# A graph network on one core: order of the fill of its edge loop, and the source one-hots made by VectorE

## What is computed

```python
edge_feat = jnp.concatenate([x[src], x[dst], edge_attr], axis=-1)
h = mish(edge_feat @ W1 + b1)          # W1: (512 + 512 + 64) x 512
messages = mish(h @ W2 + b2)           # W2: 512 x 512
agg = jax.ops.segment_sum(messages, dst, num_segments=x.shape[0])
u = mish(jnp.concatenate([x, agg], axis=-1) @ W3 + b3)
out = u @ W4 + b4                      # then layernorm(x + out) * gamma + beta
```

## Time and profile before

| | |
|---|---|
| median of 3 runs | 254.63 us (254.29 to 255.37) |
| the profiled execution | 255.16 us, of which the trace spans 253.4 us |
| PE, matmuls | 235.5 us busy (93% of the span) |
| VectorE (DVE) | 153.9 us (61%) |
| ScalarE (ACT) | 121.6 us (48%) |
| granted clock of PE, mean | 0.977 of full speed |

### The profile page before, as it was taken

The page is one execution under the profiler, slowest core; times in us unless marked ns, Lnnn a source line. Parts: engine busy times, 40 slices in busy tenths (PEclk is TensorE's granted clock), DMA queues, the critical chain, the costliest instruction groups (busy, mean ns, idle before and its releaser), DMA issues.

```text
span 253.4 us, 3283 instructions
## 1 busy us (share of the span) xinstructions
PE 235.5 (93%) x1269; PEld 189.6 (75%) x1269; DVE 153.9 (61%) x266; ACT 121.6 (48%) x221; POOL 5.6 (2%) x17
## 2 busy tenths in 40 slices
PE   7998999997998499999999999999999998999980
PEld 3967789764765378888888888888888887986760
DVE  3977875336877335585675856758568355264625
ACT  0415399779267614553654735647455343150000
POOL 0000100001000000000000000000000000000001
PEclk9999999999999679999999999999999999999996
DMA  6999983501930000004505031040000000000001
GB/s 214 319 415 414 406 319 132 168 0 35 281 101 0 0 0 0 3 0 134 197 3 166 0 111 60 0 166 0 0 3 0 0 0 0 3 0 0 3 0 43
DMA packets 12991, 23.39 MB, mean 92 GB/s; under 512 B 920, under 2 KB 3888, under 8 KB 12848
## 3 DMA queue, kind: packets, MB, share of 16 engines
q1 hardware_dynamic: 12336, 22.81, 25.7%
q10 hardware_dynamic: 640, 0.37, 0.6%
HBM read 22.92 MB, written 0.26 MB: 91 GB/s over the span
## 4 chain that ended last, share of the span: by engine, by line
PE 82%; DVE 8%; issue 4%; ACT 4%; POOL 1%; POOLq 0%; DVEq 0%
PE bank L625 33%; PE bank L610 12%; PE bank L432 8%; PE bank L441 5%; PE bank L488 4%; PE bank L635 3%; PE bank L636 3%; PE bank L451 2%; ACT C L281 2%; DVE Sbf L829 2%; DVE Dbf L829 2%; PE bank L421 1%; PE bank L646 1%; PE bank L463 1%; PE bank L415 1%
## 5 line engine op out<-in xcount | busy, mean ns | idle before, releaser
L625 PE MATMUL bank<-W2hi,Hhi 128*128 128x512 f32 x128 | 51.1, 399 | 4.2 <-issue 4.2
L625 PE MATMUL bank<-W2lo,Hhi 128*128 128x512 f32 x128 | 50.9, 398 | 0.0
L625 PE MATMUL bank<-W2hi,Clo 128*128 128x512 f32 x128 | 50.8, 397 | 0.0
L365 ACT ACTIVATE Mhi<-M 128x512 fp32r<-128x512 f32 x32 | 20.2, 632 | 50.6 <-DVE M L933 50.6
L938 DVE TENSOR_TENSOR Mlo<-M,Mhi 128x512 fp32r<-128x512 f32 x32 | 22.1, 689 | 24.4 <-ACT M L366 24.4
L933 DVE TENSOR_TENSOR M<-bank,b2r 128x512 f32<-128x512 f32 x32 | 22.0, 687 | 17.8 <-PE bank L625 9.2
L625 PEld LDWEIGHTS bank<-W2hi,Hhi 128*128 128x128 f32 x128 | 24.7, 193 | 9.8 <-issue 4.6
L625 PEld LDWEIGHTS bank<-W2hi,Clo 128*128 128x128 f32 x128 | 24.7, 193 | 5.2
L625 PEld LDWEIGHTS bank<-W2lo,Hhi 128*128 128x128 f32 x128 | 24.7, 193 | 5.2
L358 ACT ACTIVATE Hhi<-C 128x512 fp32r<-128x512 f32 x32 | 20.0, 624 | 14.7 <-DVE C L919 14.4
L924 DVE TENSOR_TENSOR Clo<-C,Hhi 128x512 fp32r<-128x512 f32 x32 | 22.0, 688 | 6.6 <-ACT C L359 6.5
(11 more groups left out here) (178 smaller groups left out, 315.9 us busy)
## 6 DMA issues: line engine op xcount, KB each, us to landing
F<-in_L_gnn_W SPq DMA_DIRECT2D x2, 2048.0 KB, 13.3
W1raw<-in_L_gnn_W SPq DMA_DIRECT2D x1, 2048.0 KB, 20.9
W<-in_L_gnn_W SPq DMA_DIRECT2D x1, 2048.0 KB, 8.9
Wq<-in_L_gnn_Wq SPq DMA_DIRECT2D x2, 512.0 KB, 5.0
Wk<-in_L_gnn_Wk SPq DMA_DIRECT2D x2, 512.0 KB, 7.7
Wv<-in_L_gnn_Wv SPq DMA_DIRECT2D x1, 1024.0 KB, 11.8
ea<-in_edge_attr SPq DMA_DIRECT2D x1, 1024.0 KB, 12.5
Wo<-in_L_gnn_Wo SPq DMA_DIRECT2D x1, 1024.0 KB, 15.3
```

Of the source, the lines that this page charges most:

```text
L365: act.activation(Mhi[:, t, :], M[:, t, :], ACT.Mish)
L625: done = mm(ST2[t][:, :], x[:, c, e], w[:, c, :], start=c == 0 and i == 0, stop=c == KC - 1 and i == 2)
```

## The change

It does six things.

1. PE no longer turns the source one-hots (32 matmuls L463) and ScalarE no longer moves them (8 moves L295). Instead a DMA brings the 4096 source ids to all 128 partitions (`srow`, 128 x 4096 int32, 2048 KB), and VectorE compares them with the partition's number, in four instructions of 1024 elements, one ahead of each two remainders of W1. The view that it reads steps over 32 ids from one element to the next, since edge e*32 + t belongs to partition e of tile t.
2. `srow` lies in units 0 to 7 of the region, where Wq and Wk lay, and where `C` will lie. So SP waits for `qk_ready` before it goes on, and ScalarE waits for all four compares (`st_ready`) before its first move of an edge term.
3. SP's order: the three rows b2, g2, be2 before W1raw, then `srow`; W2raw right after F2.
4. On PE an edge step moves ahead of the feed-forward's last part (steps 3 to 5 there, 6 to 10 behind).
5. In the fill ScalarE runs `hidden` of group 0 whole, then the late steps 13 to 15, then `hidden` of group 1; `W2hi` comes after step 11. VectorE's `z1_out`, `hidden_low` and the four remainders of W2 are interleaved anew.
6. The second layer's group 0 waits for late moves by tile: six of eight for tiles 0 and 1, all eight for 2 and 3.

```diff
-        DT_UNIT, ST_UNIT, C_UNIT = 0, G, 2 * G
+        DT_UNIT, C_UNIT = 0, G
@@ SyncE
-            sp.dma_start(W1raw, w_view(a["L1_gnn_W1"][0:2 * D, :])).then_inc(S["w1_in"], 16)
+            sp.wait_ge(S["qk_ready"], 2 * KC)
             for name in EARLY_ROWS[4:]:
                 load_row(name)
-
-            sp.wait_ge(S["pre_done"], ST_UNIT)
+            sp.dma_start(W1raw, w_view(a["L1_gnn_W1"][0:2 * D, :])).then_inc(S["w1_in"], 16)
+            sp.dma_start(other["srow"], by_partition(a["src"], E)).then_inc(S["srow_in"], 16)
+
+            sp.wait_ge(S["pre_done"], C_UNIT)
             sp.wait_ge(S["ct_done"], 1)
             sp.dma_start(F2, w_view(a["L0_gnn_W2"])).then_inc(S["f2_in"], 16)
-            sp.wait_ge(S["pre_done"], C_UNIT)
             sp.dma_start(W2raw, w_view(a["L1_gnn_W2"])).then_inc(S["w2_in"], 16)
@@ ScalarE
                 relu_out(i)
-                onehot_out(ST, ST_UNIT, 2 * i)
-                onehot_out(ST, ST_UNIT, 2 * i + 1)
             features_high(3)
-            edge_term_out(range(3))
+            act.wait_ge(S["st_ready"], PAIRS)
+            edge_term_out(range(RING_STEPS))
@@ TensorE
-                turn_onehots(Sbf, ST_UNIT, (2 * i, 2 * i + 1))
...
-            edge_term(range(3, 5))
+            edge_term(range(3, 6))
...
+                    else:
+                        pe.wait_ge(S["late_read"], 6 if t < 2 else 8)
...
-            pe.wait_ge(S["late_read"], 2 * KC)
@@ VectorE
+            dve.wait_ge(S["srow_in"], 16)
             for c in range(2 * KC):
+                if c % 2 == 0:
+                    v.tensor_scalar(ST_by_tile[:, c // 2], srow[:, c // 2], iota_col[:, 0:1], None, ALU.is_equal).then_inc(S["st_ready"], 1)
                 dve.wait_ge(S["w1_hi"], c // 2 + 1)
```

More of the change, by code:

```diff
@@ L97, in gnn_kernel @@
         other = overlay(("Dbf", 28, 4, BF16), ("Sbf", 52, 4, BF16), ("W1hi", 56, 8, F32R), ("W1lo", 64, 8, F32R),
-                        ("Wclo", 77, 1, F32R), ("xhi", 78, 1, F32R), ("xlo", 79, 1, F32R))
+                        ("srow", 0, 8, I32), ("Wclo", 77, 1, F32R), ("xhi", 78, 1, F32R), ("xlo", 79, 1, F32R))
         low = overlay(("Clo", 0, 32, F32R), ("Mlo", 64, 4, F32R))
@@ L121, in gnn_kernel @@
         ST, DT = edge["ST"], edge["DT"]
+        ST_by_tile = ST.rearrange("p (q o i e) -> p q i o e", q=PAIRS, o=2, i=GT)
+        srow = other["srow"].rearrange("p (e q i o) -> p q i o e", q=PAIRS, o=2, i=GT)
         W2hi, W2lo = chunks(edge["W2hi"], KC), chunks(edge["W2lo"], KC)
@@ L166, in gnn_kernel @@
         S = {}
-        for name in ("x_in ids_in vecs_in ea_in wq_in0 wq_in1 wk_in0 wk_in1 wv_in wo_in f1_in f2_in w1_in wc_in w2_in w3_in w4_in g_in ws_in wn_in b1g_in "
+        for name in ("x_in ids_in srow_in st_ready vecs_in ea_in wq_in0 wq_in1 wk_in0 wk_in1 wv_in wo_in f1_in f2_in w1_in wc_in w2_in w3_in w4_in g_in ws_in wn_in b1g_in "
                      "out_stored consts ident_ready ident_bf_ready x_transposed xT_ready cols_done cols_ready q_done k_done v_done "
@@ L344, in _ @@
                 relu_out(i)
-                onehot_out(ST, ST_UNIT, 2 * i)
-                onehot_out(ST, ST_UNIT, 2 * i + 1)
             features_high(3)
-            edge_term_out(range(3))
+            act.wait_ge(S["st_ready"], PAIRS)
+            edge_term_out(range(RING_STEPS))
             act.wait_ge(S["w2_in"], 16)
             act.activation(W2hi[:, :, :], W2raw, ACT.Copy).then_inc(S["w2_hi"], 1)
-            edge_term_out(range(3, KC * PAIRS - 3))
+            edge_term_out(range(RING_STEPS, RING_STEPS + 1))
             def hidden(g, j):
@@ L366, in message @@
                 act.activation(M[:, t, :], M[:, t, :], ACT.Mish).then_inc(S["m_hi"], 1)
-            for j in range(3):
+            for j in range(KC):
                 hidden(0, j)
[L370 to L377, removed]
+            edge_term_out(range(RING_STEPS + 1, KC * PAIRS))
+            for j in range(KC):
+                hidden(1, j)
             for g in range(G):
@@ L574, in _ @@
             columns_by((bank[1], bank[2]), ffT, F2, 1, range(FC - 2), 0, FC - 1)
-            edge_term(range(3, 5))
+            edge_term(range(3, 6))
             for h in range(2):
                 columns_by((bank[1], bank[2]), ffT, F2, h, range(FC - 2, FC), 0, FC - 1).then_inc(S["f2_done"], 1)
-            edge_term(range(5, RING_STEPS - 1))
+            edge_term(range(6, RING_STEPS - 1))
             pe.wait_ge(S["graph_ready"], 2)
@@ L647, in turn @@
                 done.then_inc(S["wt_done"], 1)
+            pe.wait_ge(S["st_ready"], PAIRS)
             pe.wait_ge(S["ab_ready"], 2)
@@ L877, in _ @@
             out_halves(xT_flat, (bank[1], bank[2]), S["nT_done"], 0, S["nT_ready"])
-            dve.wait_ge(S["nx_ready"], 2)
-            chain(v.tensor_tensor(xw[:, :], y[:, :], r("L0_gnn_b2"), ALU.add))
             features_low(1)
             features_low(2)
+            dve.wait_ge(S["srow_in"], 16)
             for c in range(2 * KC):
+                if c % 2 == 0:
+                    v.tensor_scalar(ST_by_tile[:, c // 2], srow[:, c // 2], iota_col[:, 0:1], None, ALU.is_equal).then_inc(S["st_ready"], 1)
                 dve.wait_ge(S["w1_hi"], c // 2 + 1)
@@ L888, in _ @@
             v.tensor_copy(Cn[:, :], bank[4][:, N:2 * N]).then_inc(S["graph_ready"], 1)
+            dve.wait_ge(S["nx_ready"], 2)
+            chain(v.tensor_tensor(xw[:, :], y[:, :], r("L0_gnn_b2"), ALU.add))
             xb = r("L0_gnn_be2")
@@ L901, in _, with w2_low @@
             out_halves(xT_flat, xs_banks, S["nT_done"], 2, S["nT_ready"])
-            dve.wait_ge(S["w2_hi"], 1)
-            for c in range(KC):
-                v.tensor_tensor(W2lo[:, c, :], W2raw[:, c, :], W2hi[:, c, :].bitcast(F32), ALU.subtract).then_inc(S["w2_lo"], 1)
+            def w2_low(cs):
+                dve.wait_ge(S["w2_hi"], 1)
+                for c in cs:
+                    v.tensor_tensor(W2lo[:, c, :], W2raw[:, c, :], W2hi[:, c, :].bitcast(F32), ALU.subtract).then_inc(S["w2_lo"], 1)
             dve.wait_ge(S["ab_done"], 1)
@@ L908, in _ @@
             v.tensor_tensor(Alo, bank[1][:, :], Ahi.bitcast(F32), ALU.subtract).then_inc(S["ab_ready"], 1)
+            w2_low((0, 1))
             dve.wait_ge(S["ab_done"], 2)
@@ L946, in one_hot @@
                                 iota_row[:, :].unsqueeze(1).to_broadcast([P, GT, N]), ALU.is_equal).then_inc(S["m_oh"], 1)
[L948 to L955, removed]
+            for j in range(KC):
+                z1_out(0, j)
+            w2_low((2,))
+            for j in range(KC):
+                hidden_low(0, j)
+                z1_out(1, j)
+                if j == 0:
+                    w2_low((3,))
+            for j in range(KC):
+                hidden_low(1, j)
             for g in range(G):
```

## The result

| | before | after |
|---|---|---|
| median | 254.53 us (254.29 to 255.37, 4 runs) | 250.91 us (250.34 to 251.83, 4 runs) |
| profiled execution, its span | 255.16 us, 253.4 us | 250.34 us, 248.5 us |
| granted clock, mean | 0.977 | 0.994 |

The ratio is 0.9855, 95% interval 0.9818 to 0.9893: faster by about 3.6 us. The forecast was 256.7 us, slower than before, and its range began at 252.0.

The account below looks back on a forecast made before the run. PE, busy 93% of the span, bounds the kernel; transposes +6.3, idle time -4.2, its clock -3.0, new clock loss +3.0 make +2.1 us: 257.3 profiled, 256.7 median, range 252.0 to 259.4.

Parts of the forecast that it names:

- the clock's price in the feed-forward: PE idles 5.1 us before edge step 2, so its clock falls to half speed there, costing 3.0 us.
- wait before the second layer: PE's 4.19 us of idle time ahead of the second layer goes, and the 3.0 us of halved clock with it.
- The compares, the disputed price: VectorE's four compares ahead of `st_ready`: 2.2 us each, between ends of 1.2 and 2.8.
- the upper end: Highest price of one VectorE compare: eight times a 128-word PSUM row of 350 ns, 2.8 us.
- the clock's +3.0: Clock loss expected after PE's 5.1 us of idle time before edge step 2: 3.0 us added.
- the step is free: Rival: stepped reads cost VectorE's compares nothing, 1.2 us each, transposes only 2.3 later, 249.7 us; chance 18%.
- The estimate of 1.85 us: Lower figure for one VectorE compare by the skill page's stream prices, which gave 1.85 to 2.64 us.
- the fill: Reordering before the second layer removes 4.2 us of PE idle time and 3.0 of halved clock: -7.2 us.
- the queue: SP's transfers: `srow` lands at 40.8, F2 behind it at 46.0, so PE idles 3.1 us before F2.
- the 1.8 us of turns left out: PE's dropped turns of ST bring it to F2's matmuls 1.8 us earlier, but this is not gained.

Follow-up runs that it names:

- e4_step_prices: Changed kernel plus 22 VectorE instructions of 1024 elements (11 forms, each twice) behind its last layernorm; 283.55 us, which means nothing as a time.
- e5_compares_twice: Changed kernel with each compare run a second time into unused memory, and all eight waited for; 256.52 us, ratio 1.0084.
- e1_fill_alone: Kernel before with only parts 5 and 6, the fill reordered, `W2hi` left where it was; 248.38 us, ratio 0.9768.
- e2_onehots_alone: Changed kernel with the fill put back to the old order, one-hots by VectorE and SP's new order kept; 257.70 us, ratio 1.0133.
- e11_step_behind: Changed kernel with part 4 undone, edge step 5 back behind the feed-forward's last part; 250.75 us, ratio 0.9849.
- e3_read_without_step: Changed kernel with compares reading neighbouring words of `srow` instead of every 32nd; 251.78 us, ratio 0.9895.

## Why the prediction was wrong

Step by step, forecast against the profile after:

| | forecast | measured |
|---|---|---|
| `srow` lands, F2 lands | 40.8, 46.0 | 40.4, 45.4 |
| one compare | 2.2 | 1.09 to 1.15 |
| `st_ready` complete | 53.5 | 48.2 |
| PE idle before F2, before step 2 | 3.1, 5.1 | 2.54, 0.47 |
| step 2 | 54.7 | 49.65 |
| transposes | 68.7 (+6.3) | 64.43 (+2.1) |
| the clock's price in the feed-forward | 3.0 | none |
| wait before the second layer | none | none |

**The step that failed is "The compares, the disputed price."** It named both ends rightly, 1.2 and 2.8 us, then took 2.2, "because where its words come from visibly slows this operation". The measured 1.1 is at the lower end, even 0.1 below it. The rows used for the upper end compare small instructions, 128 words from PSUM against 256 from SBUF, and most of such a row seems not to be its stream: by `e4_step_prices` 1024 words from SBUF take 0.75 us, far less than four times the 411 ns of 256. If the two kinds of row are alike, some 0.44 ns a word and 0.3 us an instruction are an estimate from these two numbers. Then that end was not a bound from a near row but for the most part a start-up cost multiplied by eight.

The error of 1.1 us counts fourfold, and then once more through the clock. Step 2 starts 5.05 us earlier than forecast; 4.4 of that are the four compares and 0.4 is the landing. PE's idle time there shrinks to 0.47, so the clock's +3.0 goes as well. Together: forecast +2.1; the transposes +2.1 instead of +6.3 and 3.0 of clock less give -5.1. `e5_compares_twice` shows the other side of it: put the price back, and step 2, the lost clock and the forecast's time are measured, the last with some luck. The rival "the step is free" forecast 249.7 by the same steps and had 18%. It came closest to the time, 1.2 under the median; its name is wrong, since the step costs 0.34 us of 1.09.

The Trainium skill ("VectorE: DVE Perf Modes", section "Mode 2×_2P — use both read ports for one tensor") says that an instruction with one source in SBUF can stream it over both read ports, in f32 too, and that one with two sources cannot. The runs agree: 0.75 against 1.22 us for 1024 words. The forecast scaled a two-operand remainder and missed this.

The Trainium skill ("Vector Engine (DVE) Microarchitecture Reference", section 5.2), which the forecast weighed, has its table from a program with two sources. For two sources stepping 24 words `e4_step_prices` gives 2.72 us for 1024, 2.66 ns a column where the page has 2.50: near. For one source at 32 words the runs give 1.09 us, 1.06 ns a column, not the page's 1.73 for one of two sources that hops. The estimate of 1.85 us came from carrying that line over to an instruction of another kind, and it lies 0.75 above what was measured.

**Right:** the fill. The 4.19 us are gone, the clock holds, and `e1_fill_alone` measures 6.2 of 7.2 by the medians and 7.1 by the profiles. The forecast was made against a profiled execution 0.5 above its median with a mean clock of 0.977; the seven runs of before beside `e1_fill_alone` had 0.982 to 0.989. In `e2_onehots_alone`, at 0.988, the same stall cost 1.7 of clock instead of 3.0. So a usual execution of before probably has less clock to win, which fits the missing 1.0; their stretches were not recorded. **Right too:** the queue, within 0.6 us, and that the 1.8 us of turns left out would be lost in F2's wait.

**Missed, small:** behind step 2 the transposes took 14.8 us, not 14.0. Of the 0.8, half is the feed-forward, out at 58.74, 9.1 us behind step 2 instead of 8.7. The other half lies behind it, where the forecast counted layernorm as the limit; the chain goes over ScalarE's moves and edge step 10 instead. And the clock's price after a fall is not a constant: 3.0 us before the second layer in the profile of before, 1.7 at the same place in `e2_onehots_alone`, 1.7 in the feed-forward.

## What to carry to other kernels

Where one unknown price is multiplied and also decides whether there is an idle time that can cost the clock, forecast the two outcomes with their own sums; a middle value between far ends can be the least likely of all. Bound the price of a long instruction by long rows with as many operands; short rows multiplied can hold the start-up cost many times over. A change of several parts wants each part run alone, for here all of the gain comes from the order of the fill, and the rest gives 2.2 to 2.5 us of it back (ratios 0.9768 against 0.9855, medians 248.38 against 250.91 us): some 0.6 by part 4, and most by a transfer of 2048 KB, behind which both the compares and F2 have to wait.

## What the runs showed of the hardware

- VectorE's price of a step depends on its length and is not the dearer the longer: one source of 1024 words takes 0.75 us unstepped, 1.14 at 8 words, 1.49 at 24, 1.13 at 31, 1.09 at 32. A stepped write costs the same as a stepped read: 1.50 at 24 and 1.10 at 32. With two sources: 1.22, then 2.72 at 24 and 1.89 at 32 (all from `e4_step_prices`).
- The same idle time does not always cost the clock, and not even its length orders the cases. Ahead of F2, PE idled for over 2 us in six profiles. The clock held after 2.26 us (`e2_onehots_alone`), 2.54 (the changed kernel), 3.09 (`e5_compares_twice`) and 3.10 (`e11_step_behind`); it was low after 2.85 (`e3_read_without_step`) and after only 2.28 in `e4_step_prices`, which is the changed kernel up to its last layernorm. The two ends, `e11_step_behind`:

```profile
46.11 2.86 PE L429 MATMUL bank<-F,ffT 128*128 128x256 f32 x12 [3.10 <-DMA F<-in_L_gnn_W]
```

```profile
46.00:48.00 2.00, 1.89 (x9) 1.00 0.31 120
```

and `e4_step_prices`:

```profile
45.40 4.54 PE L429 MATMUL bank<-F,ffT 128*128 128x256 f32 x12 [2.28 <-DMA F<-in_L_gnn_W]
```

```profile
46.00:48.00 2.00, 2.00 (x7) 0.59 0.20 78
```

After 4.19, 4.20 and 4.57 us (before, `e2_onehots_alone`, `e5_compares_twice`) it was low each time.
- The landing of the same transfer moved by 1.0 us between executions: `srow` between 40.25 and 41.29 in seven profiles.
